# Other places for the side work in the table that orders the rounds of a graph network kernel

## The chip, the cores and the metric

The kernel runs on one core of a Trainium2 chip. Its engines are TensorE (PE in the profile, PEld for its weight loads), VectorE (DVE), ScalarE (ACT), GpSimd (POOL), and SyncE (SP), which issues the DMAs. The metric is the device time in microseconds (us) of one launch.

## The reference

The input is 128 graphs of 128 nodes with 64 features, and a weighted adjacency `adj` for each graph. Layer 0 adds a masked sum over neighbours of a two-layer edge function, layer 1 a gated update; both end with a residual and a layer norm.

```python
# layer 0: for every pair of nodes, then over neighbours
mask = (adj > 0.0)
h = relu((x @ W1a)[:, :, None, :] + (x[:, :, None, :] - x[:, None, :, :]) @ W1b + b1)
hm = einsum('bjkh,bjk->bjh', h, mask)
x = layernorm(x + hm @ W2 + deg[..., None] * b2)
# layer 1
m = relu(relu(x @ W1 + b1) @ W2 + b2)
msg = relu(einsum('bij,bjh->bih', adj, m))
x = layernorm(x + gru(msg, x))      # two sigmoids, one tanh, six products
```

## The kernel before

The hidden layer has 192 channels. Work is cut into 32 quads of four graphs; two quads make a group of eight graphs, for which loads, masks and layer 1 are done. For each node the neighbours are taken one after the other, in "rounds": TensorE adds to PSUM the difference between the next neighbour's product and the last one's, and VectorE then reads the PSUM tile, clips it at zero and adds it to the sum `AC` in SBUF. A quad has nine rounds a (`round_a`, L795 and L1073; VectorE's instruction is L1083) and nine rounds b (`round_b`, L804 and L1085; VectorE's is L1094). Rounds a of quad t are interleaved with rounds b of quad t-1, as b1 a1 b2 a2 ... b9 a9, so that TensorE works on one while VectorE reads the other. Round a(n) on TensorE waits for VectorE's round a(n-1), and the same holds for b. Rounds 1 to 6 are 1152 elements wide on VectorE, 7 to 9 are 768. In each step the text calls the interleaved rounds "quad t".

All other work is put between the rounds by hand. `ORDER` (L59) has one line for even quads and one for odd; each line has 19 strings, the first before b1, then one behind b1, one behind a1, and so on. Every letter is a step, and it stands at that place in the streams of all engines that take part in it. The letters that matter here:

- `p` is the next step of `prep` (L413) for quad t+1: `ov`, `rank_t`, `rank_ov`, `words`, two `x_turn`, then `v`, `v_low` twice, then `v_out` and `surplus` together. `v` is TensorE's L723 to L729 with ScalarE's copy L1390, `v_low` is L735 with the copy L1395.
- `r` is the next step of `ranks` (L395) for a later group: `mask` (VectorE, L1009), `rank_n` twice (TensorE L662, copy L1342), `split_x`, `count` (VectorE, L1016 to L1033), `off` (TensorE L669, VectorE L1039 and L1041).
- `0` to `4` are `dgen` (L1051): VectorE makes the difference matrix `DM0` to `DM4` of the next quad from bytes (L1061, and L1064 for `DM4`). GpSimd has a `dgen` too (L1539), which issues nothing and only waits until VectorE's is done.
- `w` is `switch` (VectorE, L1070, writes `SW`), `c` is `clear` (GpSimd's memset L1530 of the outer columns of the next quad's `AC`), `s` is `seeds` (TensorE L758 and L764, ScalarE L1414, GpSimd L1537).
- `t` is the next step of `tail` for quad t-2 (`s_ov` L826, `out0_a` L838, `out0_b`, `out0_c` L855); `n`, `d` and `e` are steps of layer 1 of three groups (`squares2` on ScalarE is L1319, `power2` on GpSimd is L1471 and L1473, `tanh` L1301, `yt` L646, `xg` L582, `m1` L570 to L573); `l` loads a group.

`seeds` of quad t+1 waits on TensorE for the end of VectorE's round b9 of quad t (L753), since it writes the same PSUM banks. TensorE's b1 of the next quad stands behind it and reads `SW`. PSUM banks 6 and 7 are shared by all side work in the order in which the steps take them.

Of the kernel before, what the change touches and what calls it, by code (L numbers as in the profile page):

```python
# [56 lines left out]


ORDER = (  # L59
    ("psp23", "pd", "et", "te", "", "t", "r", "pedp", "r", "et", "erpe", "p", "ed4", "p", "re", "d", "p", "wpre0", "c1"),  # L60
    ("s2pd", "3pp", "", "t", "d", "tpp", "", "4teptn", "", "cdp", "d", "pl", "d", "wnd", "dd0p", "", "epdr", "", "d1p"),
)

LAST = (
# [1633 lines left out]
```

## Time and profile before

| | |
|---|---|
| median of 3 runs | 957.42 us (956.57 to 958.09) |
| the profiled execution | 956.57 us |
| its span | 954.9 us |
| PE busy | 859.1 us, 90% of the span |
| DVE busy | 841.1 us, 88% |
| ACT, POOL busy | 560.0 us, 305.9 us |
| instructions | 25003 |

A row of the timeline has the start in us from the span's start, the busy time in us, the engine, the line, the operation, what it writes and reads, the count, and in brackets the idle time ahead of it with what ended it. A row of the waits says who waited for whom, for how many us in total, how many times, and for how long at most. Rows of one engine can overlap by up to 0.1 us, since an instruction starts while the one before it drains.

### The profile page before, as it was taken

How to read it: one execution, taken by the hardware profiler on the slowest of the kernel's cores; microseconds unless marked ns; L12 is line 12 of the kernel's file. 1: busy time of each engine (PE TensorE's matmuls, PEld its weight loads, DVE VectorE, ACT ScalarE, POOL GpSimd, SP SyncE). 2: the span in 40 equal slices, each digit the busy share in tenths (PEclk: the TensorE clock that was granted, in tenths of full speed). 3: DMA queues.
4: the chain of work that ended last, by engine and by line, in shares of the span. 5: the costliest groups of instructions: out<-in, count | busy, mean ns of one | idle time of the engine just before them, and what ended most of it. 6: DMA issues, size and time to landing. Idle time of an engine off the chain costs nothing.

```text
span 954.9 us, 25003 instructions
## 1 busy us (share of the span) xinstructions
PE 859.1 (90%) x10132; PEld 599.0 (63%) x10132; DVE 841.1 (88%) x1055; ACT 560.0 (59%) x1627; POOL 305.9 (32%) x300
## 2 busy tenths in 40 slices
PE   2778888999999999999999999999999999999983
PEld 1445566767666666766666666766666666766652
DVE  5389999999999999999999999999999999998742
ACT  3433445576676756666666656666666657655442
POOL 1111111242423424242423424242423424142441
PEclk9779899999999999999999999999999999999986
DMA  4122121213113131312113231311213121211000
GB/s 136 27 47 78 46 78 38 70 46 84 34 39 87 46 90 29 91 46 60 48 46 90 46 89 29 90 46 44 63 45 91 45 80 40 56 45 31 1 12 23
DMA packets 31425, 53.27 MB, mean 56 GB/s; under 512 B 8137, under 2 KB 16972, under 8 KB 31308
## 3 DMA queue, kind: packets, MB, share of 16 engines
q1 hardware_dynamic: 31308, 51.65, 21.4%
q8 instruction: 81, 1.33, 0.6%
q14 instruction: 36, 0.29, 0.1%
HBM read 13.87 MB, written 4.19 MB: 19 GB/s over the span
## 4 chain that ended last, share of the span: by engine, by line
PE 69%; DVE 15%; issue 13%; ACT 1%; POOL 1%; POOLq 0%; DVEq 0%
PE PS L772 17%; PE PS L781 12%; DVE AC L1094 6%; DVE AC L1083 4%; PE PS L758 3%; PE PS L826 3%; PE PS L625 3%; PE PS L838 3%; PE PS L855 3%; PE PS L646 2%; PE PS L764 2%; PE PS L601 2%; PE PS L612 2%; PE PS L570 1%; PE PS L637 1%
## 5 line engine op out<-in xcount | busy, mean ns | idle before, releaser
L1094 DVE SCALAR_TENSOR_TENSOR AC<-PS,AC 128x1152 f32<-128x1152 f32 (+1 forms) x288 | 351.0, 1219 | 43.1 <-PE PS L772 42.9
L1083 DVE SCALAR_TENSOR_TENSOR AC<-PS,AC 128x1152 f32<-128x1152 f32 (+1 forms) x288 | 350.2, 1216 | 28.7 <-PE PS L781 17.2
L772 PE MATMUL PS<-DM,VA 128*128 128x192 fp8e5 (+1 forms) x1152 | 135.6, 241 | 19.5 <-DVE AC L1083 19.2
L772 PE MATMUL PS<-DM,VB 128*128 128x192 fp8e5 (+1 forms) x1152 | 135.8, 241 | 0.0
L781 PE MATMUL PS<-DM,VB 128*64 128x192 fp8e5 (+1 forms) x1152 | 95.6, 245 | 37.6 <-DVE AC L1094 35.2
L772 PEld LDWEIGHTS PS<-DM,VA 128*128 128x128 f16 x1152 | 87.9, 100 | 50.9 <-DVE AC L1083 37.5
L781 PEld LDWEIGHTS PS<-DM,VB 128*64 128x64 f16 x1152 | 46.8, 109 | 89.1 <-issue 43.5
L1530 POOL MEMSET AC<- 128x768 f32 x32 | 24.0, 749 | 245.5 <-DVE DM L1064 144.8
L772 PEld LDWEIGHTS PS<-DM,VB 128*128 128x128 f16 x1152 | 75.8, 98 | 37.0 <-issue 0.9
L781 PE MATMUL PS<-DM,VA 128*64 128x192 fp8e5 (+1 forms) x1152 | 98.8, 252 | 0.0
L1537 POOL TENSOR_TENSOR AC<-AC,NNB 128x512 f32<-128x512 f32 x64 | 66.1, 1052 | 68.3 <-ACT AC L1414 37.4
L781 PEld LDWEIGHTS PS<-DM,VA 128*64 128x64 f16 x1152 | 40.9, 109 | 41.3 <-issue 31.9
L1061 DVE TENSOR_SCALAR DM<-CW 128x1536 uint16<-128x1536 uint16 (+1 forms) x132 | 66.7, 537 | 0.0
L1384 ACT ACTIVATE XE<-PS 128x512 f16<-128x512 f32 x64 | 37.8, 592 | 43.3 <-PE PS L713 43.3
L1390 ACT ACTIVATE VN<-PS 128x384 f16<-128x384 f32 x64 | 31.3, 488 | 49.6 <-PE PS L729 49.6
L1342 ACT ACTIVATE Q<-PS 128x512 bf16<-128x512 f32 x32 | 19.0, 597 | 63.6 <-PE PS L662 63.6
L1395 ACT ACTIVATE VN<-PS 128x384 f16<-128x384 f32 x64 | 31.4, 490 | 41.8 <-PE PS L735 41.7
L1526 POOL TENSOR_TENSOR XHL<-XN,XHL 128x512 f16<-128x512 f32 x16 | 18.6, 1161 | 81.1 <-ACT XHL L1347 81.1
L1367 ACT ACTIVATE AM<-PS 64x512 int16<-64x512 f32 x64 | 37.7, 589 | 10.5 <-PE PS L683 10.1
L838 PE MATMUL PS<-w2s,AC 128*128 128x64 f32 x256 | 40.1, 289 | 0.0
L826 PE MATMUL PS<-w2s,AC 128*64 128x64 f32 x1024 | 36.8, 225 | 0.0
L838 PEld LDWEIGHTS PS<-w2s,AC 128*128 128x128 f32 x256 | 36.5, 191 | 0.0
(221 smaller groups left out, 1849.6 us busy)
## 6 DMA issues: line engine op xcount, KB each, us to landing
CW<-WM SPq DMA_DIRECT2D x128, 160.0 KB, 2.9
AT<-in_adjt SPq DMA_DIRECT2D x16, 512.0 KB, 4.6
VA<-VN SPq DMA_DIRECT2D x64, 96.0 KB, 2.2
VB<-VN SPq DMA_DIRECT2D x64, 96.0 KB, 2.2
XN<-in_xn SPq DMA_DIRECT2D x16, 256.0 KB, 4.7
out<-YO SPq DMA_DIRECT2D x15, 256.0 KB, 4.6
cs<-in_cst SPq DMA_DIRECT2D x1, 550.5 KB, 3.5
out<-YO SPq DMA_DIRECT2D x2, 128.0 KB, 1.7
```

Of the source, the lines that this page charges most:

```text
L772: last = e.matmul(PS[:, b + i % 2, 256 * (i // 2) + cols.start:256 * (i // 2) + cols.stop], lhs[:, GRAPH[i], 0:128], d[:, i, :], start=Fal ...
L781: last = e.matmul(PS[h, b + 2, 256 * (i // 2) + cols.start:256 * (i // 2) + cols.stop], lhs[:, GRAPH[i], 128:H], d[:, i, :], start=False, ...
L826: last = e.matmul(PS[64 * h:64 * h + 64, b, 64 * i:64 * i + 64], ac[:, n, c:c + 64], w2s[:, w, :], start=(w == 0), stop=(w > 0))
L838: e.matmul(o, ac[:, i % 2, 256 * (i // 2) + 64:256 * (i // 2) + 192], w2s[:, 0, :], start=False, stop=True, skip_group_check=True)
L1061: e.tensor_scalar(d, w[:, halves, first], 6 - 2 * m, 0xC0C0, ALU.logical_shift_left, ALU.bitwise_and).then_inc(s["dd"], 1)
L1083: e.scalar_tensor_tensor(dst, tiles(PS[:, b:b + 3, :])[:, :, cols], 0.0, dst, ALU.max, ALU.add).then_inc(s["sx"], 1)
L1094: e.scalar_tensor_tensor(dst, tiles(PS[:, b:b + 3, :])[:, :, cols], 0.0, dst, ALU.max, ALU.add).then_inc(s["sy"], 1)
L1367: e.activation(graphs(am[k])[:, :, 64 - 64 * h:192 - 64 * h], src[k], ACT.Copy, scale=2.0, bias=-258.0)
L1384: e.activation(XE[q % 4][:, 2 * k:2 * k + 2, :].rearrange("p i n -> p (i n)"), PS[:, b, :], ACT.Copy).then_inc(s["xe"], 1)
L1390: e.activation(VN[q % 2][:, 0, 2 * k:2 * k + 2, :], PS[:, b, :].rearrange("p (a n) -> p a n", a=2)[:, :, 0:H], ACT.Copy).then_inc(s["vh"], 1)
L1395: e.activation(VN[q % 2][:, 1, 2 * k:2 * k + 2, :], PS[:, b, :].rearrange("p (a n) -> p a n", a=2)[:, :, 0:H], ACT.Copy).then_inc(s["vl"], 1)
L1537: e.tensor_tensor(t[:, h, nat], t[:, h, nat], NNB[q % 2][:, h, :], ALU.mult).then_inc(s["im"], 1)
```

## The change

Only the two lines of `ORDER` are changed; `LAST`, which orders the last two quads, and all steps stay as they are. No instruction is added or taken away.

```diff
 ORDER = (
-    ("psp23", "pd", "et", "te", "", "t", "r", "pedp", "r", "et", "erpe", "p", "ed4", "p", "re", "d", "p", "wpre0", "c1"),
-    ("s2pd", "3pp", "", "t", "d", "tpp", "", "4teptn", "", "cdp", "d", "pl", "d", "wnd", "dd0p", "", "epdr", "", "d1p"),
+    ("ps2p3", "pe", "t", "t", "", "dtr", "e", "pdrpe", "", "ert", "pee", "ep", "4d", "p", "pre", "", "cwpd", "r", "e01"),
+    ("sp2d3", "pp", "", "t", "d", "tpp", "", "4tept", "n", "dp", "d", "p", "dc", "nld", "d0wpd", "", "epd", "p", "d1r"),
 )
```

In even quads both `rank_n` stand one place earlier (the second now just ahead of `x_turn`), the second `v` stands behind a7 where it stood behind a8, `v_low` and `switch` stand ahead of b9, `m1` moves from ahead of a8 to ahead of b9, `clear` moves ahead of b9 too, and `DM0` to `DM3` are made behind a9 in one run. In odd quads `mask` moves behind a9, `surplus` ahead of it, and `switch` behind the making of `DM0`.

The end of an odd quad on VectorE, from round b8 on. L1094 is a round b, L1083 a round a, L1009 the mask, L1061 a difference matrix. Before:

```order
729 L1094 SCALAR_TENSOR_TENSOR AC<-PS,AC 128x6x128
730 L1083 SCALAR_TENSOR_TENSOR AC<-PS,AC 128x6x128
731 L1009 TENSOR_SCALAR MT<-AT 128x1024
732 L1094 SCALAR_TENSOR_TENSOR AC<-PS,AC 128x6x128
733 L1083 SCALAR_TENSOR_TENSOR AC<-PS,AC 128x6x128
734 L1061 TENSOR_SCALAR DM<-CW 128x1536 x3
735 L1094 SCALAR_TENSOR_TENSOR AC<-PS,AC 128x6x192
```

The same place on VectorE in the changed kernel:

```order
716 L1094 SCALAR_TENSOR_TENSOR AC<-PS,AC 128x6x128
717 L1083 SCALAR_TENSOR_TENSOR AC<-PS,AC 128x6x128
718 L1094 SCALAR_TENSOR_TENSOR AC<-PS,AC 128x6x128
719 L1083 SCALAR_TENSOR_TENSOR AC<-PS,AC 128x6x128
720 L1061 TENSOR_SCALAR DM<-CW 128x1536
721 L1009 TENSOR_SCALAR MT<-AT 128x1024
722 L1061 TENSOR_SCALAR DM<-CW 128x1536 x2
723 L1094 SCALAR_TENSOR_TENSOR AC<-PS,AC 128x6x192
```

The mask has left the place ahead of b9 and stands between the matrices that are made ahead of the next b1.

The end of an even quad on VectorE, from round b8 on, before. L1070 is the switch, L1039 and L1041 are `off`:

```order
701 L1094 SCALAR_TENSOR_TENSOR AC<-PS,AC 128x6x128
702 L1083 SCALAR_TENSOR_TENSOR AC<-PS,AC 128x6x128
703 L1094 SCALAR_TENSOR_TENSOR AC<-PS,AC 128x6x128
704 L1070 TENSOR_SCALAR SW<-CW 128x512
705 L1039 TENSOR_TENSOR SI<-iot,PS 128x1024
706 L1041 COPY VE<-PS 128x16
707 L1061 TENSOR_SCALAR DM<-CW 128x1536
708 L1083 SCALAR_TENSOR_TENSOR AC<-PS,AC 128x6x128
709 L1061 TENSOR_SCALAR DM<-CW 128x1536 x2
710 L1094 SCALAR_TENSOR_TENSOR AC<-PS,AC 128x6x192
711 L1061 TENSOR_SCALAR DM<-CW 128x1536
```

The end of an even quad on VectorE in the changed kernel:

```order
690 L1094 SCALAR_TENSOR_TENSOR AC<-PS,AC 128x6x128
691 L1083 SCALAR_TENSOR_TENSOR AC<-PS,AC 128x6x128
692 L1070 TENSOR_SCALAR SW<-CW 128x512
693 L1094 SCALAR_TENSOR_TENSOR AC<-PS,AC 128x6x128
694 L1039 TENSOR_TENSOR SI<-iot,PS 128x1024
695 L1041 COPY VE<-PS 128x16
696 L1083 SCALAR_TENSOR_TENSOR AC<-PS,AC 128x6x128
697 L1061 TENSOR_SCALAR DM<-CW 128x1536 x4
698 L1094 SCALAR_TENSOR_TENSOR AC<-PS,AC 128x6x192
```

The switch now stands ahead of b9, and the four matrices in one run between a9 and the next b1.

GpSimd from `split_xg` of an even quad to the seeds, with the semaphores that each instruction waits for (`dd` counts VectorE's matrices), before:

```order
162 L1522 TENSOR_TENSOR XGl<-XG,XGh 128x512 [waits gate,xgc]
163 L1471 TENSOR_SCALAR st<-st 128x8 [waits lny,sqy,dd]
164 L1473 TENSOR_TENSOR st<-st 128x8 [waits powy]
165 L1530 MEMSET AC 128x6x2x64 [waits o0,dd]
166 L1537 TENSOR_TENSOR AC<-AC,NNB 128x4x128 [waits ini,nnc,dd]
```

GpSimd at the same place in the changed kernel:

```order
162 L1522 TENSOR_TENSOR XGl<-XG,XGh 128x512 [waits gate,xgc,dd]
163 L1471 TENSOR_SCALAR st<-st 128x8 [waits lny,sqy]
164 L1473 TENSOR_TENSOR st<-st 128x8 [waits powy]
165 L1530 MEMSET AC 128x6x2x64 [waits o0]
166 L1537 TENSOR_TENSOR AC<-AC,NNB 128x4x128 [waits nnc,ini,dd]
```

The instructions are the same, but the memset no longer waits for a matrix: it follows `power2` as soon as `out0_c` of an old quad is done.

## Rows read from the trace of the kernel before

**Rows 1.** The page, busy time, share of the span and instructions of two engines.

```profile
PE 859.1 (90%) x10132; PEld 599.0 (63%) x10132; DVE 841.1 (88%) x1055; ACT 560.0 (59%) x1627; POOL 305.9 (32%) x300
```

**Rows 2.** The waits: waiting engine, releaser, us in total, times, longest.

```profile
DVE AC L1094 <- PE PS L772: 42.9, 84, 2.9
...
PEld PS L758 <- DVE AC L1094: 5.2, 15, 0.4
```

**Rows 3.** The timeline of VectorE, end of odd quad 17, start of quad 18.

```profile
515.74 0.68 DVE L1009 TENSOR_SCALAR MT<-AT 128x1024 bf16<-128x1024 f32 x1
516.34 0.95 DVE L1094 SCALAR_TENSOR_TENSOR AC<-PS,AC 128x768 f32<-128x768 f32 x1
...
518.07 1.49 DVE L1061 TENSOR_SCALAR DM<-CW 128x1536 uint16<-128x1536 uint16 x3
520.37 1.36 DVE L1094 SCALAR_TENSOR_TENSOR AC<-PS,AC 128x1152 f32<-128x1152 f32 x1 [0.81 <-PE PS L772]
```

**Rows 4.** The timeline of TensorE in the same stretch: b9, `ov`, `seeds`.

```profile
515.47 0.30 PE L781 MATMUL PS<-DM,VB 128*64 128x128 fp8e5 x4
...
516.95 0.38 PE L676 MATMUL PS<-SI,shf 128*128 128x512 bf16 x1
517.34 0.61 PE L758 MATMUL PS<-XE,wxh 128*128 128x256 f16 x4
```

**Rows 5.** The timeline of VectorE, end of even quad 16, start of quad 17.

```profile
487.64 0.95 DVE L1083 SCALAR_TENSOR_TENSOR AC<-PS,AC 128x768 f32<-128x768 f32 x1
488.54 0.96 DVE L1094 SCALAR_TENSOR_TENSOR AC<-PS,AC 128x768 f32<-128x768 f32 x1
489.41 0.28 DVE L1070 TENSOR_SCALAR SW<-CW 128x512 bf16<-128x512 uint16 x1
...
493.81 1.36 DVE L1094 SCALAR_TENSOR_TENSOR AC<-PS,AC 128x1152 f32<-128x1152 f32 x1 [0.64 <-PE PS L772]
```

**Rows 6.** The timeline of TensorE in even quad 16: a7, `v`, b9, `seeds`.

```profile
483.31 0.40 PE L772 MATMUL PS<-DM,VA 128*128 128x128 fp8e5 x4 [0.15 <-DVE AC L1083]
...
486.18 0.34 PE L723 MATMUL PS<-br,on 128*128 128x384 bf16 x1
...
487.87 0.30 PE L781 MATMUL PS<-DM,VB 128*64 128x128 fp8e5 x4 [1.03 <-DVE AC L1094]
...
489.69 0.27 PE L758 MATMUL PS<-XE,wxh 128*128 128x256 f16 x1
```

**Rows 7.** The timeline of ScalarE in even quad 16: four squares of `squares2`, copy of `v`.

```profile
483.93 0.26 ACT L1319 ACTIVATE SY<-Y 128x64 bf16<-128x64 f32 x1
...
484.79 0.20 ACT L1319 ACTIVATION_READ_ACCUMULATOR SY<-Y 128x1 f32 x1
...
486.88 0.49 ACT L1390 ACTIVATE VN<-PS 128x384 f16<-128x384 f32 x1 [0.37 <-PE PS L729]
```

**Rows 8.** The timeline of GpSimd in even quad 16: `power2`, `clear`, `seeds`.

```profile
485.42 1.65 POOL L1473 TENSOR_TENSOR st<-st 128x8 f32<-128x8 f32 x1
491.44 0.74 POOL L1530 MEMSET AC<- 128x768 f32 x1 [4.37 <-DVE DM L1061]
492.79 2.20 POOL L1537 TENSOR_TENSOR AC<-AC,NNB 128x512 f32<-128x512 f32 x2 [0.61 <-DVE DM L1061]
```

**Rows 9.** The timeline of GpSimd in the first 30 us.

```profile
8.79 1.20 POOL L1526 TENSOR_TENSOR XHL<-XN,XHL 128x512 f16<-128x512 f32 x1 [4.70 <-ACT XHL L1347]
24.74 1.09 POOL L1530 MEMSET AC<- 128x768 f32 x1 [14.75 <-DVE DM L1061]
```

**Rows 10.** The timeline of VectorE: two instructions beside those of rows 9, one of quad 16.

```profile
9.37 0.65 DVE L1030 TENSOR_SCALAR N<-NV 128x16 bf16<-128x16 bf16 x1
...
24.00 1.15 DVE L1061 TENSOR_SCALAR DM<-CW 128x768 uint16<-128x768 uint16 x4
...
486.41 0.17 DVE L1030 TENSOR_SCALAR N<-NV 128x16 bf16<-128x16 bf16 x1
```

**Rows 11.** Windows, most of quad 0: stretch, five engines' busy, granted clock, DMA.

```profile
38.00:62.00 24.00, 17.62 (x115) 9.86 (x117) 15.77 (x32) 8.00 (x17) 3.08 (x3) 0.50 0.25 52
```

## The prediction

> **What bounds the kernel now.** The page comes first: TensorE is busy for 90% of the span and VectorE for 88% [rows 1]. Two engines that hand each other work can both be that full only if neither has much to give, so the second view is the waits: VectorE's rounds b wait 42.9 us in total for TensorE's L772, and TensorE waits 15 times for VectorE ahead of `seeds`, one time for each pair of quads [rows 2]. The timelines of both engines, read side by side over one pair (quads 16 and 17), then show who is late at each place. The pattern repeats: an odd quad's b1 and the next odd quad's b1 are about 54.1 us apart all through the middle. From a2 to a8 of an even quad VectorE runs with no gap and TensorE waits for it, 1.03 us ahead of b9 alone [rows 6]. From `seeds` of the even quad through the whole odd quad to a2 of the next even quad TensorE has hardly a gap, and VectorE waits, 0.64 us ahead of b1 of quad 17 and 0.81 us ahead of b1 of quad 18 [rows 3, 5]. The path changes engine at two places: at the end of each quad `seeds` starts just when VectorE's b9 has ended (516.34 + 0.95 = 517.29, start 517.34 [rows 3, 4]; 488.54 + 0.96 = 489.50, start 489.69, behind `surplus` [rows 5, 6]). So the end of VectorE's b9 is what this change is about: each tenth of a microsecond there is a tenth of a pair, once for each pair.
>
> **Odd quads: the mask leaves the place ahead of b9.** The mask takes 516.34 - 515.74 = 0.60 us of VectorE ahead of b9 [rows 3]. Without it b9 can start as soon as TensorE's b9 is ready: TensorE starts it at 515.47 [rows 4], and in quad 16 the start-to-start distance from TensorE's b9 to VectorE's is 488.54 - 487.87 = 0.67 [rows 5, 6], which gives 516.14, and an end at 517.09. TensorE itself is free for `seeds` only when `ov` is through: `ov` starts at 516.95 [rows 4], takes some 0.22, so 517.17. `surplus` moves ahead of a9, but it is the same TensorE work before the same `seeds`. Gain: 517.34 - 517.17 = 0.17 us. VectorE must now fit the mask between a9 and b1: three matrices from 518.07 to 519.56 and the mask's 0.60 end near 520.05 (a9 itself comes 0.1 earlier), and b1 starts at 520.37 [rows 3], 520.20 with the gain. It fits by 0.15 to 0.25 us. Masks stand in odd quads up to 27: twelve quads (5 to 27) give 12 x 0.17 = 2.0 us. In quads 1 and 3 TensorE has no layer 1 work, the mask alone holds `seeds` up, and I take 0.5 of its 0.6 us each: 1.0 us.
>
> **Even quads: switch and clear.** `switch` (start to start 489.61 - 489.41 = 0.20, since the rows overlap; busy 0.28 [rows 5]) moves ahead of b9. Alone it is nearly free: VectorE leaves a8 at 487.64 + 0.87 = 488.51, the switch ends the slot at 488.71, and b9 starts there and not at 488.54. Its end, 489.67, is 0.03 us later than `seeds` can bear. But `clear` moves too, and on GpSimd the memset loses its wait for a matrix. Where does it land? `v` on TensorE now follows a7: 483.31 + 0.58 = 483.89. ScalarE copies it 486.88 - 486.18 = 0.70 us after its start [rows 6, 7], at 484.6, and the squares stand behind that copy, so they start at 485.0 and not at 483.93. They take 484.79 + 0.20 - 483.93 = 1.06; the long instruction of `power2` follows the last by 485.42 - 484.99 = 0.43 and takes 1.65 [rows 7, 8]. Together: 485.0 + 1.06 + 0.43 + 1.65 = 488.14. The memset follows at about 488.2 and lasts 0.74 to 488.96. VectorE issues the switch at 488.51, in the middle of it.
>
> Does that hurt? Three rows of the start say yes. L1030 is a small bf16 instruction that takes 0.17 us in quad 16 [rows 10]; beside GpSimd's L1526, which runs to 9.99, it took 0.65 and ended at 10.02 [rows 9, 10]. And a GpSimd memset of 0.74 took 1.09 beside a run of four matrices [rows 9, 10]. The switch has the matrices' kind of operands (16 bit in, 16 bit out, one scalar operation on SBUF). So VectorE would wait from 488.51 to the memset's last 0.1 us, near 488.84: 0.33 more, b9 starts at 489.04, ends at 490.0, and `seeds` starts at 490.05 against 489.69: a loss of 0.36 us. The bounds are 0.03 (no overlap, or no blocking) and 0.49 (held to the memset's very end, and a tail of 0.03). I take 0.36, since the overlap of 0.45 us is larger than the error of my chain, some 0.2. It needs `power2` and `count` in the same quad, as in the even quads 6 to 28: 12 x 0.36 = 4.3 us, with bounds of 0.4 and 5.9.
>
> The Trainium skill, "SBUF — State Buffer", section "SBUF: two separate sides", states that GpSimd and a VectorE instruction in a two-port mode share one pair of ports, and that the one that starts first holds it for its whole instruction. The case of L1030 at 9.37 fits; the row at 486.41 does not, since it took 0.17 us in the middle of `power2`'s 1.65 us. By the page to the letter `power2` would block as well as the memset; by the rows only a long stream does, and the memset is one.
>
> **The other moves.** `rank_n` directly ahead of `x_turn` makes TensorE wait for ScalarE's copy (0.6 us) with a4 queued behind it; `words` stands in the same slot on VectorE and gives 0.74 us of cover, and my chain reaches a4 0.2 us before VectorE wants it. The delay runs on through b5 and a5 to b6, where before TensorE was just in time: I take 0.03 us (0 to 0.15) x 12 = 0.4 us. `v` between a7 and b8 fills 0.5 us that TensorE idled; `v_low` and `m1` ahead of b9 fill the 1.03 us [rows 6], so they cost nothing, but gain nothing either, because a9 waits for VectorE's a8 in both orders. In quad 2 the early `v_low` no longer waits for its copy: a gain of 0.3. Moving `DM0` and `DM3` changes nothing as long as the run of four is done before b1 (493.6 against 493.81 [rows 5]); in the blocked case b1 comes later too. SP's queue keeps its order of transfers. In quad 0 there are no rounds b to hide anything: `rank_n` now stands ahead of a3 on TensorE and waits for the mask (0.68 us), so a3 comes up to 0.9 us later, at the clock of 0.50 (1.2 GHz) that the row shows for 38 to 62 us [rows 11]. Part of it comes back before b1 of quad 1, if the clock rises at the same time as before: 0.4 to 0.9, taken as 0.6.
>
> **The sum.** -2.0 (odd quads) - 1.0 (quads 1 and 3) + 4.3 (even quads) + 0.4 (`x_turn`) - 0.3 (quad 2) + 0.6 (quad 0) = +2.0 us. The profiled execution took 956.57 (span 954.9 and 1.7 around it), which gives 958.6. It was the fastest of three, 0.85 below the median; on the median of 957.42 the sum is 959.4, and I say 959.3. A measurement of this kernel can tell a change from none at about 0.2%, or 1.9 us, so the forecast sits on that line.
>
> **The rivals.** First, the memset misses the switch, or does not hold VectorE up: the even term is 0.4 and not 4.3, the sum -1.9, the time 955.5. For it speaks that my chain for `power2` adds six durations, and 0.3 us of error moves the memset clear of the switch; that a memset only writes; and that `power2` did not block L1030. It decides from 0.33 us of blocking: below about 0.15 us per pair, the change is a gain. This is the case that ends on the other side.
>
> Second, GpSimd gets in between two matrices. The four matrices now stand in one run, and the seeds' multiply on GpSimd is released by the second (492.79 before, behind the second too [rows 8]). If it starts between the third and the fourth, the fourth waits for its first half, about 1.4 us of the 2.20, b1 of the odd quad is late by over a microsecond, and TensorE's path there has no slack: 1.0 us for each of some 14 pairs, 973. Against it: the memset at 24.74 arrived in the third of four matrices and the run still took 1.15 us, as if alone, while the memset was longer by 0.35 [rows 9, 10]. The run wins. The same could happen behind the mask in odd quads, where b1's slack of 0.8 us covers most of it.
>
> Third, the wait ahead of `x_turn` is longer than I take it (another copy stands ahead on ScalarE): from 0.2 us late at a4 it passes to VectorE and costs up to 0.3 us for 12 pairs, 3.6 us on top: 963.
>
> **How the numbers follow.** Blocking as computed 0.55 (959.3, own range 957 to 961.5), no blocking 0.25 (955.5, range 954 to 957.5), GpSimd between the matrices 0.10 (973), a longer wait at `x_turn` or something unseen of that kind 0.10 (963). The range leaves out the third case and little else: 954.6 to 964.0. Slower by over 0.2%: half of the first case (0.27), and nearly all of the last two (0.18), 0.45 in all. Faster by over 0.2%: a little over half of the second, 0.16. The same: 0.39.
>
> **What the changed profile would show.** Right: ahead of b9 in even quads from 6 on the switch's row is 0.5 to 0.65 us long and not 0.28, with the memset beside it at about 488.2 in that pair's time; `seeds` of even quads starts about 0.36 later after VectorE's a8, `seeds` of odd quads 0.17 earlier after TensorE's b9; a pair takes 54.3 us and not 54.1. Wrong: a memset that ends before or starts behind the switch, or a switch of 0.28 beside it (first rival); a matrix row over 1 us, or a gap among the four (second rival); idle time of VectorE ahead of a4 or b6 of even quads above 0.1 us (third rival).

## The result, and the profile after

| | before | after |
|---|---|---|
| median (range of 4 runs each) | 957.40 us (956.57 to 958.09) | 966.81 us (965.92 to 967.65) |
| ratio, 95% interval | | 1.0099 (1.0084 to 1.0115) |
| span of the profiled execution | 954.9 us | 964.4 us |

The change makes the kernel 9.4 us slower. The page of the changed kernel, to be held against [rows 1] (busy time, share of the span, instructions):

```profile
PE 852.2 (88%) x10132; PEld 597.0 (62%) x10132; DVE 870.5 (90%) x1055; ACT 568.0 (59%) x1627; POOL 314.7 (33%) x300
```

VectorE has the same 1055 instructions and is busy for 29.4 us more; TensorE is not. So some VectorE instructions have become longer. The groups of instructions by line and shape tell which (count, busy time in us, mean ns of one). Before:

```profile
L1061 DVE TENSOR_SCALAR DM<-CW 128x1536 uint16<-128x1536 uint16 x124 | 64.3, 550 | 0.0
```

After:

```profile
L1061 DVE TENSOR_SCALAR DM<-CW 128x1536 uint16<-128x1536 uint16 x124 | 93.0, 791 | 0.0
```

The same 124 difference matrices take 28.7 us more, which is nearly the whole 29.4. The waits show nothing of it. VectorE even waits less for TensorE than in [rows 2], because the longer matrices fill time in which it idled before; what holds the matrices up counts as their busy time.

```profile
DVE AC L1094 <- PE PS L772: 21.9, 53, 2.1
```

The timeline of VectorE at the end of even quad 16 and the start of quad 17 (start, busy time), against [rows 5]:

```profile
492.79 0.41 DVE L1070 TENSOR_SCALAR SW<-CW 128x512 bf16<-128x512 uint16 x1
...
496.05 3.02 DVE L1061 TENSOR_SCALAR DM<-CW 128x1536 uint16<-128x1536 uint16 x4
499.00 1.35 DVE L1094 SCALAR_TENSOR_TENSOR AC<-PS,AC 128x1152 f32<-128x1152 f32 x1
```

GpSimd in the same stretch, against [rows 8]:

```profile
490.70 1.66 POOL L1473 TENSOR_TENSOR st<-st 128x8 f32<-128x8 f32 x1
492.31 0.73 POOL L1530 MEMSET AC<- 128x768 f32 x1
497.20 2.46 POOL L1537 TENSOR_TENSOR AC<-AC,NNB 128x512 f32<-128x512 f32 x2 [4.15 <-DVE DM L1061]
```

Four matrices take 3.02 us, where four alone take 1.95 (the first experiment shows it). A window that begins inside the last of them shows it by itself:

```profile
497.46 1.62 DVE L1061 TENSOR_SCALAR DM<-CW 128x1536 uint16<-128x1536 uint16 x1
```

It takes 1.62 instead of 0.55. The seeds' multiply on GpSimd started at 497.20, in the third matrix, and got in ahead of the fourth. The fourth is 1.07 us longer, a little less than the 1.27 us that the first of GpSimd's two multiplies takes alone. No semaphore ties the two: in the kernel's text a matrix waits for a DMA and for counts of TensorE alone. The text below says "the port" for whatever VectorE's matrices and GpSimd's instructions can't use at the same time. b1 of quad 17 no longer waits for TensorE (0.64 us before [rows 5]) but starts behind the matrices. At the end of odd quad 17 the same happens behind the mask, against [rows 3]:

```profile
521.32 0.96 DVE L1094 SCALAR_TENSOR_TENSOR AC<-PS,AC 128x768 f32<-128x768 f32 x1 [0.33 <-PE PS L772]
...
523.56 0.69 DVE L1009 TENSOR_SCALAR MT<-AT 128x1024 bf16<-128x1024 f32 x1
524.16 2.10 DVE L1061 TENSOR_SCALAR DM<-CW 128x1536 uint16<-128x1536 uint16 x2
526.17 1.34 DVE L1094 SCALAR_TENSOR_TENSOR AC<-PS,AC 128x1152 f32<-128x1152 f32 x1
```

The ends of quads 1 to 28 all show it, 28 of 28, by 1.07 to 1.08 us. A pair of quads takes 54.89 us instead of 54.11, from a1 of one even quad to a1 of the next. By stretches of that pair: from a2 of an even quad to b1 of the odd one 23.65 instead of 22.80 (+0.85); from b8 of the odd quad to b1 of the next even one +0.63; from there to a2 of that quad -0.70, since VectorE idled there before. So the end of the even quad costs time, and what the end of the odd quad loses comes back, with 0.07 us on top. Up to quad 4 both kernels stand at the same time (a1 at 143.2 us in both), at a1 of quad 30 the changed one is 9.6 us behind.

### The profile page after: what moved, and what is told of

Same layout as the page of the kernel before. It is cut to its first block, busy times and chain, and to the rows that moved or that the text cites. A ratio compares the mean times of both kernels' runs of the same rounds, so it can differ in the third digit from the quotient of the medians.

```text
span 964.4 us, 24987 instructions
## 1 busy us (share of the span) xinstructions
PE 852.2 (88%) x10132; PEld 597.0 (62%) x10132; DVE 870.5 (90%) x1055; ACT 568.0 (59%) x1627; POOL 314.7 (33%) x300
## 4 chain that ended last, share of the span: by engine, by line
PE 59%; DVE 23%; issue 14%; ACT 2%; POOL 1%; POOLq 0%; DVEq 0%
PE PS L772 15%; PE PS L781 11%; DVE AC L1094 8%; DVE AC L1083 5%; DVE DM L1061 4%; PE PS L826 3%; PE PS L625 3%; PE PS L838 3%; PE PS L855 3%; PE PS L646 2%; PE PS L758 2%; DVE SI L1039 2%; PE PS L612 2%; PE PS L570 1%; PE PS L637 1%
## 5 line engine op out<-in xcount | busy, mean ns | idle before, releaser
L1083 DVE SCALAR_TENSOR_TENSOR AC<-PS,AC 128x1152 f32<-128x1152 f32 (+1 forms) x288 | 350.0, 1215 | 28.3 <-PE PS L781 19.4
L1094 DVE SCALAR_TENSOR_TENSOR AC<-PS,AC 128x1152 f32<-128x1152 f32 (+1 forms) x288 | 350.1, 1216 | 23.6 <-PE PS L772 21.9
L1537 POOL TENSOR_TENSOR AC<-AC,NNB 128x512 f32<-128x512 f32 x64 | 76.9, 1221 | 125.4 <-DVE DM L1061 68.7
L1061 DVE TENSOR_SCALAR DM<-CW 128x1536 uint16<-128x1536 uint16 (+1 forms) x132 | 95.4, 764 | 0.0
L1522 POOL TENSOR_TENSOR XGl<-XG,XGh 128x512 f16<-128x512 f32 x15 | 17.4, 1160 | 78.8 <-DVE DM L1064 78.8
```

Source lines behind the costliest of these rows:

```text
L1061: e.tensor_scalar(d, w[:, halves, first], 6 - 2 * m, 0xC0C0, ALU.logical_shift_left, ALU.bitwise_and).then_inc(s["dd"], 1)
L1083: e.scalar_tensor_tensor(dst, tiles(PS[:, b:b + 3, :])[:, :, cols], 0.0, dst, ALU.max, ALU.add).then_inc(s["sx"], 1)
L1094: e.scalar_tensor_tensor(dst, tiles(PS[:, b:b + 3, :])[:, :, cols], 0.0, dst, ALU.max, ALU.add).then_inc(s["sy"], 1)
L1537: e.tensor_tensor(t[:, h, nat], t[:, h, nat], NNB[q % 2][:, h, :], ALU.mult).then_inc(s["im"], 1)
```

## The experiments

"Before" and "after" name the two kernels. Each edit stands as a diff. What is added or moved is all that differs.

**The multiply behind all matrices.** After, with a wait in GpSimd's `seeds`, so that the multiply cannot meet a matrix:

```diff
                 po.wait_ge(s["nnc"], q + 1)
+                po.wait_ge(s["dd"], RD * q + 4)
```

> The changed kernel, with one wait more on GpSimd: the seeds' multiply (L1537) starts only when all four matrices of its quad are made. Port theory (the multiply gets in between two of VectorE's matrices and stops the next one for its first half): rows of L1061 go back from 3.02 us for four and 2.10 for two to 1.95 and 1.01, VectorE's busy time falls by about 28 us, a pair takes 54.0 to 54.1 us and not 54.9, and the time is 955.5 to 958.5 us. Theory that the side work moved within even quads costs the time (rank_n ahead of x_turn, v behind a7, m1 ahead of b9): stays at 965 to 967. Theory of the switch behind the memset: stays at 965 to 967 too.

Measured: 959.18 us (958.79 to 960.95), ratio to before 1.0031 (1.0020 to 1.0043). The run of four on VectorE, and the a1 behind it, at the end of quad 16:

```profile
492.71 1.95 DVE L1061 TENSOR_SCALAR DM<-CW 128x1536 uint16<-128x1536 uint16 x4
...
497.01 1.36 DVE L1083 SCALAR_TENSOR_TENSOR AC<-PS,AC 128x1152 f32<-128x1152 f32 x1 [0.76 <-POOL AC L1538]
```

The multiply beside no matrix:

```profile
494.92 1.97 POOL L1538 TENSOR_TENSOR AC<-AC,NNB 128x512 f32<-128x512 f32 x2 [5.21 <-DVE DM L1061]
```

The run is down from 3.02 to 1.95 and the multiply from 2.46 to 1.97, and two thirds of the loss are gone (1.0099 to 1.0031) with an added wait and no other edit. I had expected all of it (955.5 to 958.5, a pair of 54.0 to 54.1), and the pair is 54.40. The rest fits the idle time in the second row, a price of the added wait: a1 now waits 0.76 us for the later multiply.

**Each line of the table alone.** On before, first the odd line of after, then the even one:

```diff
-    ("s2pd", "3pp", "", "t", "d", "tpp", "", "4teptn", "", "cdp", "d", "pl", "d", "wnd", "dd0p", "", "epdr", "", "d1p"),
+    ("sp2d3", "pp", "", "t", "d", "tpp", "", "4tept", "n", "dp", "d", "p", "dc", "nld", "d0wpd", "", "epd", "p", "d1r"),
```

> The kernel before with the odd line of the changed table alone (mask behind a9, surplus ahead of it, switch behind DM0, and DM3 ahead of b1 of the odd quad). Port theory: the multiply still meets DM2 and DM3 back to back at both ends of quads, so a pair loses 0.6 to 0.9 us: 964 to 969 us. Theory of the side work in even quads, and that of the switch and the memset: nothing of it is in this kernel, 955 to 957.5 us.

> The kernel before with the even line of the changed table alone. DM3 stands behind b1 of the odd quad as before, so no matrix follows another while the multiply waits. Port theory: 957 to 960 us (0.13 us for each pair from the switch behind the memset, up to 0.9 us in quad 0). Theory of the side work in even quads, and that of the switch and the memset: 965 to 968 us.

Measured: the odd line alone 967.37 us (964.27 to 967.81), ratio 1.0100 (1.0081 to 1.0120); the even line alone 958.0 us (957.04 to 958.4), ratio 1.0013 (1.0003 to 1.0022). The odd line brings the whole loss. Its first string, with `3` moved ahead of b1, makes the run at the end of the even quad one matrix longer, and that is the matrix that the multiply gets ahead of. The timeline of VectorE and of GpSimd with the odd line alone, end of quad 16:

```profile
498.25 2.56 DVE L1061 TENSOR_SCALAR DM<-CW 128x1536 uint16<-128x1536 uint16 x3
...
498.88 2.51 POOL L1537 TENSOR_TENSOR AC<-AC,NNB 128x512 f32<-128x512 f32 x2 [0.61 <-DVE DM L1061]
```

Three matrices take 1.49 alone [rows 3]. All the side work of even quads (the earlier `rank_n`, `v`, `m1`, switch and memset) together costs 0.1 us per pair (54.20), so neither the blocked switch nor the wait at `x_turn` is the cause of the 9.4 us.

**The run of four on before.** Only the matrices move:

```diff
-    (..., "p", "wpre0", "c1"),
-    ("s2pd", "3pp", ...
+    (..., "p", "wpre", "0c1"),
+    ("s2p3d", "pp", ...
```

> The kernel before, with only DM0 moved behind a9 and DM3 ahead of b1 at the end of even quads, so that four matrices stand in one run; all else stays. Port theory: the run takes 3.0 us and not 1.95, b1 of odd quads starts about 0.8 us later, 0.8 for each of 14 pairs: 966 to 969 us. Both other theories: 957 to 957.5 us, as before.

Measured: 976.83 us (974.44 to 976.97), ratio 1.0211 (1.0194 to 1.0228), more than the 966 to 969 expected. VectorE and GpSimd at the end of quad 16:

```profile
499.83 3.64 DVE L1061 TENSOR_SCALAR DM<-CW 128x1536 uint16<-128x1536 uint16 x4
503.39 1.34 DVE L1094 SCALAR_TENSOR_TENSOR AC<-PS,AC 128x1152 f32<-128x1152 f32 x1
```

```profile
500.44 1.08 POOL L1530 MEMSET AC<- 128x768 f32 x1 [5.23 <-DVE DM L1061]
501.49 2.56 POOL L1537 TENSOR_TENSOR AC<-AC,NNB 128x512 f32<-128x512 f32 x2
```

The run takes 1.69 us longer than 1.95: here the memset too, which still waits for a matrix, gets in, ahead of the third (0.62), and the multiply ahead of the fourth (1.07). In the changed kernel the early `clear` kept the memset away; of the two GpSimd instructions it met only one.

**The multiply in smaller pieces.** After, with the first multiply cut in halves, so that GpSimd has three multiplies of 256 elements for two of 512 and 256:

```diff
+                    if k == 0:
+                        f = slice(0, 2)
+                        e.tensor_tensor(t[:, f, nat], t[:, f, nat], NNB[q % 2][:, f, :], ALU.mult)
+                        h = slice(2, 4)
                     e.tensor_tensor(t[:, h, nat], t[:, h, nat], NNB[q % 2][:, h, :], ALU.mult).then_inc(s["im"], 1)
```

> The changed kernel with one edit: the first of the two GpSimd multiplies of the seeds (512 elements, 1.23 us) is cut into two of 256; the second stays whole. Theory: GpSimd gets the shared port between two of VectorE's matrices and holds it for one of its own instructions only. The block is then as long as the shorter multiply: the run of four takes about 2.5 us instead of 3.02 (1.95 + 0.6), the run of two about 1.6 instead of 2.10, and b1 of odd quads comes some 0.5 us earlier, 14 times: 966.8 - 7 = 960, at most 963. Rival: VectorE is shut out until GpSimd has nothing more to do, or is slowed evenly while GpSimd works. Then the run of four stays at 3.0 us or grows with the extra instruction, and the time is 966 to 969.

Measured: 956.31 us (955.51 to 957.77), ratio to before 1.0001 (0.9991 to 1.0011). The end of quad 16:

```profile
491.56 2.48 DVE L1061 TENSOR_SCALAR DM<-CW 128x1536 uint16<-128x1536 uint16 x4
493.96 1.34 DVE L1094 SCALAR_TENSOR_TENSOR AC<-PS,AC 128x1152 f32<-128x1152 f32 x1
```

```profile
492.70 0.92 POOL L1539 TENSOR_TENSOR AC<-AC,NNB 128x256 f32<-128x256 f32 x1 [4.15 <-DVE DM L1061]
493.58 1.73 POOL L1541 TENSOR_TENSOR AC<-AC,NNB 128x256 f32<-128x256 f32 x2
```

The block is 0.53 us instead of 1.07: VectorE waits for one GpSimd instruction, and has the port again at its end, while GpSimd has more to do. An instruction more on GpSimd takes the whole loss away. At the end of the even quad b1 comes 0.31 us later than before for a block of 0.53, and 0.85 later for one of 1.07 in the changed kernel: 0.22 us of either are covered by what is left of VectorE's wait for TensorE ahead of b1. At the end of the odd quad 0.25 us come back, and only 0.07 in the changed kernel, with its longer block. The pair is 54.17. I had expected 960; half the block costs less than half.

**The matrices at the end of even quads spread again.** After, with these two edits:

```diff
-    (..., "cwpd", "r", "e01"),
-    ("sp2d3", "pp", ...
+    (..., "cwpd", "r0", "e1"),
+    ("sp2d", "3pp", ...
```

> The changed kernel, with the matrices at the end of even quads spread as before (one behind off, two behind a9, one behind b1); the end of odd quads, the switch, the memset, the mask and all else stay as changed. Theory: the loss sits at the end of even quads, where b1 waits for the run of four. There the rows should read as in the kernel before (L1061 alone 0.55, then two in 1.02). At the end of odd quads the two matrices behind the mask still take 2.1 us with the multiply beside them, and b1 of even quads is late, but a1, b2 and a2 take that up. The pair is about 54.1 us and the time 955 to 959. Rival: both ends cost about the same, half of the loss each: 961 to 963, the pair 54.5.

Measured: 955.79 us (955.01 to 957.45), ratio 0.9991 (0.9981 to 1.0000). The odd end stays blocked (two matrices in 2.09 us behind the mask in quad 17), and the loss is gone all the same; the pair is 54.14. The place of the loss is the end of even quads, as expected. From b8 of the odd quad to b1 of the even one it takes 7.00 us instead of 6.37, and from there to a2 4.06 instead of 4.76.

**The mask, without a block.** On before, the mask behind a9 and the third matrix behind b1:

```diff
-    ("psp23", "pd", ...
-    (..., "epdr", "", "d1p"),
+    ("psp2", "3pd", ...
+    (..., "epd", "", "dr1p"),
```

> The kernel before with two edits in the order: in odd quads the mask leaves the place ahead of b9 and stands directly behind a9, and the third of the three matrices there goes behind b1 of the even quad. Between a9 and b1 VectorE then has mask, matrix, matrix. Theory: the multiply asks some 1.4 us after a9's end, so it meets the second matrix, which has no matrix behind it before b1; the matrix behind b1 comes when the multiply is nearly through. No row is blocked by more than 0.3 us, seeds of odd quads start 0.17 us earlier, and the time is 953.5 to 956. Rival: what the mask gave at b9 comes back at a1, which has 0.46 us more of work ahead of it while TensorE's a2 waits for it, or the multiply gets in ahead of the last matrix (its row 1.6 instead of 0.55): 957 to 962.

Measured: 956.58 us (955.44 to 957.7), ratio 1.0001 (0.9991 to 1.0011): no gain. It is neither the 953.5 to 956 of the theory nor the 957 to 962 of the rival, but the rival's reason fits. The pair is 54.11, as before: 0.2 us less from a1 even to a1 odd, 0.2 more from there to a1 even. VectorE in the stretch:

```profile
519.71 1.02 DVE L1061 TENSOR_SCALAR DM<-CW 128x1536 uint16<-128x1536 uint16 x2
521.41 1.36 DVE L1094 SCALAR_TENSOR_TENSOR AC<-PS,AC 128x1152 f32<-128x1152 f32 x1 [0.68 <-PE PS L772]
522.68 0.69 DVE L1061 TENSOR_SCALAR DM<-CW 128x1536 uint16<-128x1536 uint16 x1
523.29 1.34 DVE L1083 SCALAR_TENSOR_TENSOR AC<-PS,AC 128x1152 f32<-128x1152 f32 x1
```

Nothing is blocked by more than 0.14 (0.69 for 0.55), and what b9 gained is spent by the matrix ahead of a1: b1 of the even quad starts 0.19 earlier in the pair than before and a1 0.20 later.

**The first quad's memset, earlier.** On before:

```diff
             do("dgen", 0, 0)
-            do("dgen", 0, 1)
             do("clear", 0)
+            do("dgen", 0, 1)
```

> The kernel before; only in the prologue, the first memset of GpSimd is let go by the first run of matrices of the first quad rather than by the second, so that it asks for the port about 1.1 us earlier beside that run. In the kernel before it met the last of four matrices (24.00, 1.15 us for four of 768). Theory: if it arrives with a matrix still to follow, it gets in between: the run of four 768-wide matrices takes 1.7 to 1.8 us and not 1.15, and the memset's own row is at most 0.9 us. Rival, the reading of the prediction (the run wins): the run stays at 1.15 and the memset's row grows to 1.3 or more. It happens once in the program, so the time is 956 to 958 either way.

Measured: 956.63 us in one run. VectorE and GpSimd:

```profile
24.06 1.15 DVE L1061 TENSOR_SCALAR DM<-CW 128x768 uint16<-128x768 uint16 x4
```

```profile
24.46 1.43 POOL L1530 MEMSET AC<- 128x768 f32 x1 [14.42 <-DVE DM L1061]
```

My theory failed here, and the prediction's reading held: the memset is there in the second matrix, two more follow, and none is held up; the memset ends 0.68 us behind the run (24.46 + 1.43 = 25.89; 24.06 + 1.15 = 25.21). In the kernel before, the memset came 0.73 us behind the start of the run, here 0.40, and both times it ends 0.68 us behind the end of the run; so it waited for the whole run and was not just slow to begin. The row of the first quad was no misreading, and yet every such collision in the middle of the program shows the opposite.

**A table of collisions at the end.** Before, with 15 runs of matrices on scratch space appended; each has one GpSimd instruction let go by its first, second or last matrix:

```diff
+            for c, (count, rows, cols, _, _) in enumerate(PORT):
+                ve.wait_ge(s["pb"], c + 1)
...
+                    e.tensor_scalar(d, w, 6 - 2 * (m % 4), 0xC0C0,
+                                    ALU.logical_shift_left, ALU.bitwise_and).then_inc(s["pa"], 1)
```

> The kernel before with a table of collisions appended at its end, on scratch space: 15 runs of VectorE matrices (768, 2x384, 2x512, 1280 or 2x768 elements, four or eight in a run), each with one GpSimd instruction (memset of 768, multiply of 512, pow or memset of 8) let go by the first, second or last matrix. It settles why the memset of the first quad waited for the whole run of 768-wide matrices (its row 1.43 us, the run 1.15), while in the middle of the program GpSimd gets in between matrices of 2x768. Theory A, duration: the short matrices (0.29 us) follow one another too closely; then every run of 768, contiguous or 2x384, keeps GpSimd out (4 x 768 in 1.15, 8 x 768 in 2.3 us, memset row above 1.4), and runs of 2x768 grow by 0.6 (memset) and 1.1 (multiply). Theory B, form: the contiguous ones keep GpSimd out at any length (1280 too), the 2x384 let it in. Theory C, operation: the memset waits and the multiply gets in, in both forms; but then 2x768 with the memset stays at 1.95. Theory D, place: what was seen in the first quad does not repeat, and GpSimd gets in everywhere. The pow and the memset of 8 elements should cost a matrix 0.1 us or less if the port is held only for what is written.

Measured: 994.24 us in one run, which holds the added work. Rows of the fourth collision, four matrices of 1536 with a multiply of 512: the third matrix alone, and the multiply.

```profile
957.84 1.40 DVE L1203 TENSOR_SCALAR DM<-CW 128x1536 uint16<-128x1536 uint16 x1
```

```profile
957.60 1.22 POOL L1575 TENSOR_TENSOR NNB<-NNB 128x512 f32<-128x512 f32 x1 [1.30 <-DVE DM L1203]
```

In each of the eleven collisions with a memset of 768 or a multiply of 512, the matrix behind the one in which GpSimd's instruction started is longer: by 0.62 to 0.63 us for the memset, 0.84 to 0.87 for this multiply. It is so for 768, 2x384, 2x512, 1280 and 2x768 elements and for runs of four and eight, though 768 follow one another every 0.27 us. Theory D holds; duration, form and operation are out. No matrix inside such a run waits for a semaphore of GpSimd. `pow` on 8 elements takes 1.81 us, and the four matrices of its run are 0.55 to 0.56 each; the memsets of 8 elements hold nothing up either.

**The same collisions at two places.** Before, with a table of seven collisions ahead of the first matrices and again at the end, and the first quad's memset early:

```diff
+            do("ports", 0)
             do("dgen", 0, 0)
-            do("dgen", 0, 1)
             do("clear", 0)
+            do("dgen", 0, 1)
...
+            do("ports", 1)
```

> The kernel before with the same table of seven collisions at two places: in the prologue right ahead of the first matrices, and at the end; behind the first table the first quad's memset is let go by the first of its four 768-wide matrices, as in the kernel with the early memset. In the table of the end every GpSimd instruction got in between two matrices, contiguous 768 too, but in the first quad the memset lost to the whole run. If it is the strided form of that memset, the rows with it stay at 1.15 for four matrices at both places and the memset takes 1.4 us. If it is the place (the prologue), all rows of the first table stay at 1.15 (or 1.95 for 2x768). If it is that this memset is the first GpSimd instruction in 14 us, only the first collision of the first table is of that kind, and the others, and the first quad's memset behind it, get in: a matrix of 0.97 us instead of 0.35.

Measured: 979.67 us in one run, with the added work. The first two collisions of the prologue are the same instructions. GpSimd's two rows:

```profile
25.18 1.36 POOL L1584 MEMSET AC<- 128x768 f32 x1 [14.42 <-DVE DM L1199]
27.05 0.82 POOL L1584 MEMSET AC<- 128x768 f32 x1 [0.51 <-DVE DM L1199]
```

and VectorE's fourth matrix in the first of them, its third in the second:

```profile
25.52 0.34 DVE L1199 TENSOR_SCALAR DM<-CW 128x768 uint16<-128x768 uint16 x1
...
27.12 0.97 DVE L1199 TENSOR_SCALAR DM<-CW 128x768 uint16<-128x768 uint16 x1
```

None of the first four is over 0.34. The first loses to the run, and ends 0.68 us behind it like the others that lost; the second gets in, like all 12 others and like the first quad's own memset behind the table, which lost in the run with the early memset. So it is not the form and not the place. The one that loses is the first GpSimd instruction behind 14.4 us without any. The idle time alone is not the reason. In the kernel with the run of four on before, the memset at the end of quad 0 came behind 14.35 us of idle time and got in all the same; GpSimd's row and the matrix behind it:

```profile
59.02 1.02 POOL L1530 MEMSET AC<- 128x768 f32 x1 [14.35 <-DVE DM L1061]
```

```profile
59.28 1.17 DVE L1061 TENSOR_SCALAR DM<-CW 128x1536 uint16<-128x1536 uint16 x1
```

What is left is that the loser is, in every trace of this case, the first GpSimd instruction of the program that meets a run of matrices. Why that should matter, or whether it is what VectorE did just ahead of that run, these runs don't tell.

**`words` in VectorE's idle time.** First on before, alone, then on the version below:

```diff
-    ("psp23", "pd", "et", "te", "", "t", "r", "pedp", ...
+    ("psp23", "pd", "pet", "te", "", "t", "r", "edp", ...
```

> The kernel before; only words (VectorE L1049, 0.74 us) of the even line moves from behind b4 into the place behind a1, where VectorE waits for TensorE (0.16 ahead of b2 and 0.38 ahead of a2). Nothing at the ends of quads is touched. If VectorE is the bound from b3 to a8 of even quads, as the page of idle times shows, it gains what fits in the idle time, up to 0.5 us per pair: 950 to 954. If TensorE takes over at once there (its rounds are just in time), no gain: 956 to 958.

Measured: 959.09 us (957.87 to 960.18), ratio 1.0014 (1.0005 to 1.0023), a little slower and above both ranges. VectorE reaches a4 and b5 0.7 us earlier and then waits 0.61 us for TensorE ahead of a5, where `yt` and `out0_c` stand between the rounds; from a1 of an even quad to a1 of the odd one it takes 28.1 us instead of 27.8. So moving the work away from VectorE's stretch without gaps gained nothing: TensorE was just in time there too.

**Both edits.** After with the matrices of even quads spread and the multiply in pieces (the two diffs above), and this with `words` behind a1:

> The changed kernel with two edits that each took its loss away: the matrices at the end of even quads spread as before, and the first multiply cut in halves. The pair was 54.14 with the first edit alone, with 27.43 of it from odd to even a1; there the halves take 0.53 us from the run of two. If b1 of even quads is the bound in that stretch, the pair comes to 53.7 and the time to 950 to 953; if TensorE's seeds and rounds bound it, the pair stays above 54.0 and the time is 954 to 956.

> The kernel of the run before this one, and words of the even line behind a1, where VectorE waited 0.2 to 0.4 us ahead of a2. Expected 0.2 to 0.5 us per pair below that run: 948 to 952. If the 0.74 us behind a1 pushes a2 and TensorE's a3 behind it, the gain is nought or a loss of up to 0.3 per pair: 952 to 958.

Measured, against the kernel before: 953.69 us (951.78 to 955.15), ratio 0.9953 (0.9939 to 0.9967), the pair 53.97; and with `words` moved 981.67 us (980.7 to 984.02), ratio 1.0256 (1.0241 to 1.0271). The first is faster than both kernels by under half a percent; its time and its pair lie between the two cases of the expectation. The second lies far outside what I expected, and for the known reason. In 12 of 32 quads GpSimd's `gd`, a subtraction that starts 0.07 us earlier, holds `words` up; quad 18, VectorE and GpSimd:

```profile
535.53 1.88 DVE L1049 TENSOR_TENSOR WM<-c,AM 128x1280 uint16<-128x1280 uint16 x1
```

```profile
535.46 1.27 POOL L1493 TENSOR_TENSOR GT<-XG,GN 128x512 f32<-128x512 f32 x1 [1.33 <-ACT GN L1301]
```

1.88 instead of 0.81, once more 1.07 us. b2 stands behind it, so TensorE waits 1.68 us for VectorE's b2 in each of these quads. All twelve lose about 1.6 us or more (29.1 us instead of 27.6 from a1 to a1), and six of them 2.7 to 3.1. In these six the granted clock falls behind that wait of TensorE. Windows ahead of it, behind it and after it in quad 18 (stretch, five engines' busy, granted clock, DMA):

```profile
536.00:539.00 3.00, 1.32 (x17) 0.94 (x16) 3.00 (x3) 0.51 (x3) 2.84 (x3) 1.00 0.17 37
539.00:542.50 3.50, 3.50 (x36) 3.01 (x34) 2.21 (x2) 0.77 (x3) 2.17 (x2) 0.57 0.64 158
542.50:545.00 2.50, 1.81 (x24) 1.32 (x20) 2.16 (x2) 1.52 (x6) 0.00 (x0) 0.92 0.00 0
```

The mean of 0.57 over 3.5 us is some 3 us at 1.2 GHz and not at 2.4. In the run where only `words` moved, on before, a1 and `gd` stand elsewhere against each other, and it took 0.81 to 0.83 in all quads.

## Why the prediction was wrong, point by point

The forecast was 959.3 us, within 954.6 to 964.0; the changed kernel takes 966.81. That both say "slower" is luck: the forecast's reason for it was the blocked switch, and the kernel with the even line alone, which has that block, is 1.2 us slower than before. The 9.4 us come from something that the sum has no term for.

**The step that failed** is the dismissal of the second rival. Its mechanism, its place and the two releasing rows were in the prediction: "If it starts between the third and the fourth, the fourth waits for its first half". It got 0.10, on the ground of one row: "the memset at 24.74 arrived in the third of four matrices and the run still took 1.15 us ... The run wins" [rows 9, 10]. The row is real, and a memset made earlier still loses there. But it is the exception: the first GpSimd instruction of the program that meets a run of matrices. In 24 of the 25 collisions of the two tables in which GpSimd's instruction is a multiply or a long memset, and at 28 of 28 ends of quads, GpSimd gets in at the end of the matrix in which it asks, and the next matrix is up to 1.08 us longer: the run of four takes 3.02 us and not 1.95. One row from the start of the program was set against a mechanism that recurs 28 times in its middle; there [rows 8] did speak: the multiply of 2.20 us beside the end of a matrix is 0.23 longer than the 1.97 it takes alone, so it met a matrix in each even quad, and only a successor was missing.

**The size of that rival.** It said 1.0 us for each of 14 pairs, 973. The block is 1.07 ("about 1.4 us of the 2.20" was too long for the first of the two multiplies). Of VectorE's 0.64 us of wait ahead of b1 the longer run itself uses up most; 0.22 is left, which is the prediction's own 493.6 against 493.81. So the end of the even quad costs 0.85, the end of the odd quad gives 0.07 back, and the price per pair is 54.89 - 54.11 = 0.78; twelve pairs from quad 4 to quad 28 make 9.4.

**The same behind the mask.** "b1's slack of 0.8 us covers most of it": the block is there in the odd quads 1 to 27 and is covered fully, by the wait ahead of b1 together with those ahead of b2 and a2; spreading the even end alone gave the time back.

**Even quads, switch and clear.** The mechanism is right and the size is not. In the even quads 6 to 28, those that the prediction names, the switch takes 0.41 instead of 0.28, not 0.61: the memset came at 492.31, directly behind the long instruction of `power2` (490.70 + 1.66 = 492.36), and VectorE's switch at 492.79, so that they overlap by 0.25 and not 0.45. `seeds` of quad 16 starts at 494.11, which is 1.31 behind a8's end (491.93 + 0.87) and was 1.18: 0.13 for the 0.36 of the sum. The even line alone has this block and costs 0.1 us per pair. By the Trainium skill, "SBUF — State Buffer", section "SBUF: two separate sides", GpSimd shares a pair of ports with VectorE instructions in a two-port mode, or with two SBUF inputs if GpSimd's own instruction reads SBUF, and whichever starts first holds the pair for its whole instruction. The traces agree within some 0.2 us for the first multiply (a block of 1.07 for 1.27 us), the memset (0.62 for 0.74) and the subtraction of `gd` (1.07 for 1.27), and not for `power2`: `pow` on 8 elements takes 1.81 us in the table and holds no matrix up.

**Odd quads, the mask.** `seeds` of quad 17 starts 522.33 - 520.65 = 1.68 behind TensorE's b9 and did 1.87 behind it: 0.19, predicted 0.17. How much of it is left at a2 depends on the block behind it: 0.07 us per pair in the changed kernel, with the full block, and 0.25 with the multiply in halves. Where the third matrix moves behind b1 instead, nothing is left. So a gain of the size of the sum's -2.0 (0.17 per pair) can be had, but not beside the full block, which the sum left out; how much of the 0.25 is the mask's own was not measured alone.

**The other moves.** The wait ahead of `x_turn` never showed on VectorE (third rival refuted: no idle time ahead of a4 or b6 of even quads). The even line alone gives +0.1 us per pair for all of it. In quad 0, from a1 to a1, the changed kernel takes 0.13 us more than before (predicted 0.6), the even line alone 0.77 more. Quads 1 and 3 show no gain (0.10 and 0.14 us more for the predicted 0.5 less each), quad 2 takes 0.33 less (predicted 0.3). But the blocks are in quads 1 to 3 as well, so these terms can't be told apart; a1 of quad 4 stands at 143.2 in both kernels.

**What the changed profile would show.** The sign for the second rival was "a matrix row over 1 us", and that is what it shows: 1.62. A pair takes 54.89 us and not the 54.3 of the forecast.

## What to carry to other kernels

Before VectorE instructions that, like these matrices, go from SBUF to SBUF are put in one run, look whether GpSimd is let go inside it: what counted here is whether another of them stands behind the one in which GpSimd starts. If so, try to end the run there, or to cut GpSimd's instruction in pieces, so that VectorE's wait for others covers the block; here each of the two took the loss away. And before one row is used against a mechanism, look for the place where the same two engines meet in every round.

## What the runs showed of the hardware

- GpSimd's instruction waits for the end of the VectorE matrix in which it starts, and then goes ahead of the matrix that is next in VectorE's order, even if they follow one another every 0.27 us. The next one is longer by 1.07 us (multiply, 512 elements of f32; 0.84 to 0.87 in the tables), 0.53 (256), 0.62 (memset of 768) or 0.30 (memset of 384). A VectorE shift of two SBUF operands (`words`) that starts 0.07 us behind GpSimd's subtraction of 512 elements is longer by 1.07 too. Then VectorE has its turn, though GpSimd has more: two pieces of a multiply cost it one piece.
- The profile shows such a wait as a longer busy time, and no idle time, on either engine: 1.62 us for a matrix of 0.55, 2.46 for multiplies of 1.97.
- f32 rounds that read PSUM (L1083, L1094) are 0.94 to 0.96 us (768 elements) with a memset or a multiply beside them, as without.
- A `pow` of 1.65 to 1.81 us on 8 elements held up neither L1030 (0.17 us) [rows 8, 10] nor the four matrices of its run in the table.
- The first GpSimd instruction of the program that meets a run of matrices waited for the whole run (it ends 0.68 us behind it), in both kernels and in every variant. It came behind 14.4 to 14.8 us without a GpSimd instruction, but another one behind 14.35 us got in. This was not expected and is not explained.
